# Step sizes of a state-space stage as two products of rounded parts, the bias added on VectorE and ScalarE

## The reference, cut to what matters

```python
xz = x @ W_in                                  # x is layer-normalised, (8, 224, 512)
xb, z = split(xz, 2)                           # 1024 columns each
xb = silu(sum(xp[:, k:k+L] * conv_w[:, k] for k in range(4)) + conv_b)
dt_low, Bm, Cm = split(xb @ W_x, [64, 80])     # 64 + 16 + 16 columns
dt = softplus(dt_low @ W_dt + b_dt)            # W_dt is (64, 1024): the step sizes
# then: a scan over time with exp(A * dt), dt * xb, B and C; the gate silu(z); W_out;
# a cross-attention layer; a mixture of four experts
```

## Time and profile before

| | |
|---|---|
| three runs, median (range) | 2560.08 us (2556.69 to 2561.12) |
| the profiled execution | 2564.23 us, of which 2562.4 between first and last instruction |
| PE, DVE, ACT, POOL busy over the span | 92%, 58%, 48%, 54% |
| mean granted clock of PE | 0.959 of full |

### The profile page before, as it was taken

How to read it: one execution, slowest core, us unless ns; L and a number is a source line. 1 busy time by engine, 2 the same in 40 slices (tenths; PEclk the granted TensorE clock), 3 DMA queues, 4 the chain that set the end, 5 groups by cost and what they waited for, 6 DMA issues and landing times. The chain is left out here.

```text
span 2562.4 us, 39583 instructions
## 1 busy us (share of the span) xinstructions
PE 2358.7 (92%) x14400; PEld 1994.0 (78%) x14400; DVE 1478.9 (58%) x2051; ACT 1223.5 (48%) x2655; POOL 1378.6 (54%) x968
## 2 busy tenths in 40 slices
PE   6999589999999998789999899885899999999997
PEld 5867389999999996557766666663789999999996
DVE  7804599999999994456666766663422232212322
ACT  4335377778777863334453444442333333323332
POOL 2414378778878783366566556652580080006586
PEclk9999789999999998889999999887899999999999
DMA  4326866666665664655545554621431031002323
GB/s 113 135 66 210 262 199 200 190 187 208 202 203 178 207 204 119 167 125 124 121 122 138 124 138 105 173 67 49 163 131 63 33 143 35 33 16 93 109 74 111
DMA packets 236116, 341.95 MB, mean 133 GB/s; under 512 B 35215, under 2 KB 164815, under 8 KB 234927
## 3 DMA queue, kind: packets, MB, share of 16 engines
q1 hardware_dynamic: 217246, 286.22, 39.5%
q0 software_dynamic: 14624, 50.40, 6.1%
q10 hardware_dynamic: 4080, 3.18, 0.5%
HBM read 212.08 MB, written 127.65 MB: 133 GB/s over the span
## 5 line engine op out<-in xcount | busy, mean ns | idle before, releaser
L975 DVE TENSOR_TENSOR_SCAN s_h<-s_decay,s_ub 128x928 f32<-128x928 f32 x256 | 527.2, 2080 | 8.2 <-PE s_ub L1004 1.6
L1015 PE MATMUL s_yps<-s_hc,identity 128*128 128x224 f32 x2016 | 424.1, 353 | 0.4
L2216 DVE TENSOR_TENSOR e_hl<-e_ps,e_hh 128x256 fp32r<-128x256 f32 x256 | 107.9, 424 | 497.1 <-ACT e_ps L2290 496.0
L894 ACT ACTIVATE s_decay<-s_dt,s_A 128x224 f32<-128x224 f32 x1024 | 388.0, 472 | 0.0
L1359 DVE TENSOR_REDUCE t_nmax<-t_ps 112x1 fp32r<-112x752 f32 x256 | 240.1, 938 | 224.8 <-PE t_ps L1700 224.2
L1015 PEld LDWEIGHTS s_yps<-s_hc,identity 128*128 128x128 f32 x2016 | 362.5, 190 | 2.2 <-POOL s_hc L839 1.7
L2289 ACT ACTIVATE e_hh<-e_ps,e_b 128x256 fp32r<-128x256 f32 x256 | 121.8, 476 | 498.3 <-PE e_ps L2325 498.1
L1315 POOL TENSOR_TENSOR t_part<-t_pT 125x672 f32<-125x672 f32 x128 | 207.1, 1618 | 271.8 <-ACT t_pT L1605 269.4
L1605 ACT ACTIVATE t_pT<-t_ps 125x448 f32<-125x448 f32 x384 | 181.1, 546 | 253.9 <-PE t_ps L1726 248.6
L839 POOL TENSOR_TENSOR s_hc<-s_h,carry 128x896 f32<-128x896 f32 x128 | 249.7, 1959 | 75.5 <-DVE s_h L975 51.9
L839 POOL TENSOR_TENSOR s_hc<-s_h,s_Cc 128x896 f32<-128x896 f32 x128 | 248.2, 1947 | 68.3 <-DVE s_h L975 49.8
(11 more groups left out here) (255 smaller groups left out, 5055.4 us busy)
## 6 DMA issues: line engine op xcount, KB each, us to landing
s_ut<-ut_d SPq DMA_DIRECT2D x192, 128.0 KB, 3.3
carry<-in_L_ffn_We POOLq DMA_DIRECT2D x24, 1024.0 KB, 5.7
t_k<-kh_d SPq DMA_DIRECT2D x64, 375.0 KB, 6.3
xs_d<-s_zero SPq DMA_DIRECT2D x30, 512.0 KB, 4.2
ut_d<-a_x SPq DMA_DIRECT2D x31, 448.0 KB, 5.5
kh_d<-s_kh SPq DMA_DIRECT2D x32, 375.0 KB, 2.8
kl_d<-s_kl SPq DMA_DIRECT2D x32, 375.0 KB, 3.3
v_d<-s_v SPq DMA_DIRECT2D x48, 250.0 KB
```

The lines of the kernel that those rows point to most:

```text
L894: ins = nc.scalar.activation(decay[:, u % 2, :, n, 2:SLOT], dts[:, u % 2].rearrange("p (s t) -> p s t", s=NSEG), ACT.Exp, scale=A[:, u % C ...
L975: nc.vector.tensor_tensor_scan(h[:, k].rearrange("p n t -> p (n t)"), decay[:, u % 2, k].rearrange("p n t -> p (n t)"), ub[:, s % 2, AT:AT ...
L1015: ins = nc.tensor.matmul(yps[:, u % 2, 0:L], ident[:], hc[:, u % 2, :, n], start=(n == 0), stop=(n == NS - 1))
```

## The change

`low_rank` now holds 128 rows: the 64 rows rounded to fp32r, and below them their rounded rests. `W_dt` is loaded twice, one copy below the other, rounded into `wdth` (128 rows); the rest of its first 64 rows is `wdtl`. A product is then two fp32r matmuls: `wdth` by all 128 rows (high x high plus high x low), and `wdtl` by the first 64. The row of ones is gone. The bias is a column for each chunk, `bdt`: it is the `bias` of the Abs on ScalarE, which makes two instructions out of one, and VectorE adds it, with the max, by two instructions in place in PSUM before the sum. Some tiles move (`wdt`, `xdbl` and the zeros for padding rows now lie in the space of x), which adds waits.

```diff
-            sp.dma_start(wdt[0:R], W_dt).then_inc(wdt_loaded, 16)
-            sp.wait_ge(wdt_zeroed, 1)
-            sp.dma_start(wdt[R:R + 1].rearrange("o (c p) -> o c p", p=P), b_dt.rearrange("p (o c) -> o c p", o=1),
-                         allow_slow_non_contiguous=True).then_inc(wdt_loaded, 16)
+            sp.dma_start(bdt[:], b_dt).then_inc(wdt_loaded, 16)
+            sp.wait_ge(zeroed, 1)
+            for n in range(2):
+                sp.dma_start(wdt[n * R:(n + 1) * R], W_dt).then_inc(wdt_loaded, 16)
...
-            nc.vector.memset(wdt[R:TT], 0.0).then_inc(wdt_zeroed, 1)
...
             dve.wait_ge(xn_done, NT)
-            nc.vector.memset(low_rank[R:R + 1], 1.0).then_inc(ones_set, 1)
+            nc.vector.memset(zeros, 0.0).then_inc(zeroed, 1)
             for n in range(UNITS):
                 convolution(n)
+            dve.wait_ge(wdt_loaded, 16 * 3)
+            nc.vector.tensor_copy(wdth[:], wdt).then_inc(wdt_high, 1)
+            dve.wait_ge(wdt_high, 1)
+            nc.vector.tensor_tensor(wdtl[:], wdt[0:R], wdth[0:R].bitcast(F32), ALU.subtract).then_inc(wdt_split, 1)
             for half in range(2):
-                dve.wait_ge(xdbl_mm, 2 * half + 2)
-                nc.vector.tensor_copy(grouped(xdbl[:, half_rows(half)]), ps[0:XR, 4 + 2 * half:6 + 2 * half, 0:GL]).then_inc(xdbl_done, 1)
+                both = ps[:, 4 + 2 * half:6 + 2 * half, 0:GL]
+                dve.wait_ge(low_high, half + 1)
+                nc.vector.tensor_tensor(grouped(low_rank[R:2 * R, half_rows(half)]), both[0:R],
+                                        grouped(low_rank[0:R, half_rows(half)].bitcast(F32)), ALU.subtract).then_inc(low_done, 1)
+                nc.vector.tensor_copy(grouped(xdbl[:, half_rows(half)]), both[0:XR]).then_inc(xdbl_done, 1)
...
             def softplus(j):
+                cs, rows = item(j)
                 dve.wait_ge(dt_mm, j + 1)
+                for i in range(2):
+                    nc.vector.tensor_scalar(ps[:, DT_BANK + i, 0:GL], ps[:, DT_BANK + i, 0:GL], bdt[:, cs.start + i:cs.start + i + 1], 0.0,
+                                            ALU.add, ALU.max).then_inc(relu_done, 1)
+                dve.wait_ge(relu_done, 2 * j + 2)
                 dve.wait_ge(ln_done, j + 1)
-                nc.vector.scalar_tensor_tensor(out=grouped(steps[j % RING]), in0=banks(DT_BANK), scalar=0.0, in1=grouped(steps[j % RING]),
-                                               op0=ALU.max, op1=ALU.add).then_inc(dt_done, 1)
+                nc.vector.tensor_tensor(grouped(steps[j % RING]), banks(DT_BANK), grouped(steps[j % RING]), ALU.add).then_inc(dt_done, 1)
 
             def turned_inputs(j):
+                if j == 1:
+
+                    dve.wait_ge(pads_stored, 16 * 8)
+                    dve.wait_ge(cs_stored, 16 * 2)
...
-                nc.scalar.activation(grouped(steps[j % RING]), banks(SIZE_BANK), ACT.Abs).then_inc(abs_done, 1)
+                c = item(j)[0].start
+                for i in range(2):
+                    nc.scalar.activation(steps[j % RING][:, i * GL:(i + 1) * GL], ps[:, SIZE_BANK + i, 0:GL], ACT.Abs,
+                                         bias=bdt[:, c + i:c + i + 1]).then_inc(abs_done, 1)
...
             for half in range(2):
-                act.wait_ge(xdbl_done, half + 1)
+                act.wait_ge(xdbl_mm, 2 * half + 2)
...
-                    ins = nc.tensor.matmul(ps[:, bank + i, 0:GL], wdt[:, c * P:(c + 1) * P], low_rank[:, rows], start=True, stop=True)
+                    of = slice(c * P, (c + 1) * P)
+                    nc.tensor.matmul(ps[:, bank + i, 0:GL], wdth[:, of], low_rank[:, rows], start=True, stop=False)
+                    ins = nc.tensor.matmul(ps[:, bank + i, 0:GL], wdtl[:, of], low_rank[0:R, rows], start=False, stop=True)
...
-            pe.wait_ge(wdt_loaded, 32)
-            pe.wait_ge(ones_set, 1)
+            pe.wait_ge(wdt_split, 1)
             pe.wait_ge(low_done, 2)
+            pe.wait_ge(xdbl_done, 2)
             pe.wait_ge(z_done, 2)
             size(0)
```

More of the change, by code:

```diff
@@ L83, in sem @@
             return sems[-1]
-        x_sb = sb("x", [TT, NT, DM])
+        with nc.sbuf_tensor("a_low_rank", [P, T], F32R) as low_rank:
+            pass
+        x_all = sb("x", [P, NT, DM])
+        x_sb = x_all[0:TT]
         xn = sb("xn", [TT, 2, DM])
@@ L100, in mamba_in @@
         wx_step, step7 = sb("wx", [P, TH]), sb("step7", [P, TH])
-        xdbl = sb("xdbl", [XR, T])
-        wdt = sb("wdt", [TT, DI])
+        wdth, wdtl, bdt = sb("wdth", [P, DI], F32R), sb("wdtl", [R, DI], F32R), sb("bdt", [P, CC])
         ps = ctx.enter_context(nc.psum_tensor("a_ps", [P, 8, 512], F32))
         wx = wx_step[:, 0:CC * XR].rearrange("p (c n) -> p c n", n=XR)
-        x_flat = x_sb[:].rearrange("p n d -> p (n d)")
-        low_rank = x_flat[:, 0:T]
-        uth, utl = (x_flat[:, T + i * UT_RING * DI:T + (i + 1) * UT_RING * DI].rearrange("p (j t) -> p j t", t=DI)
+        x_flat = x_all[:].rearrange("p n d -> p (n d)")
+        wdt, zeros = x_flat[:, T:T + DI], x_flat[0:PAD, T + DI:T + 2 * DI]
+        xdbl = x_flat[0:XR, T + 2 * UT_RING * DI - T:T + 2 * UT_RING * DI]
+        uth, utl = (x_flat[0:TT, T + i * UT_RING * DI:T + (i + 1) * UT_RING * DI].rearrange("p (j t) -> p j t", t=DI)
                     for i in range(2))
@@ L125, in mamba_in @@
         xb_stored, z_stored = sem("xb_stored"), [sem(f"z_stored{i}") for i in range(2)]
-        xdbl_mm, xdbl_done, low_done, ones_set, wdt_zeroed, cs_stored = (
-            sem(n) for n in ("xdbl_mm", "xdbl_done", "low_done", "ones_set", "wdt_zeroed", "cs_stored"))
+        xdbl_mm, xdbl_done, low_high, low_done, zeroed, wdt_high, wdt_split, cs_stored = (
+            sem(n) for n in ("xdbl_mm", "xdbl_done", "low_high", "low_done", "zeroed", "wdt_high", "wdt_split", "cs_stored"))
         bt_mm, bt_high, bt_split, bt_stored, pads_stored = (
             sem(n) for n in ("bt_mm", "bt_high", "bt_split", "bt_stored", "pads_stored"))
-        size_mm, dt_mm, abs_done, exp_done, ln_done, dt_done, u_done = (
-            sem(n) for n in ("size_mm", "dt_mm", "abs_done", "exp_done", "ln_done", "dt_done", "u_done"))
+        size_mm, dt_mm, abs_done, exp_done, ln_done, relu_done, dt_done, u_done = (
+            sem(n) for n in ("size_mm", "dt_mm", "abs_done", "exp_done", "ln_done", "relu_done", "dt_done", "u_done"))
         ut_mm, ut_high, ut_split = ([sem(f"{n}{i}") for i in range(2)] for n in ("ut_mm", "ut_high", "ut_split"))
@@ L170, in _ @@
             sp.dma_start(wx, W_x.rearrange("(c p) n -> p c n", p=P)).then_inc(wx_loaded, 16)
-            sp.dma_start(wdt[0:R], W_dt).then_inc(wdt_loaded, 16)
-            sp.wait_ge(wdt_zeroed, 1)
-            sp.dma_start(wdt[R:R + 1].rearrange("o (c p) -> o c p", p=P), b_dt.rearrange("p (o c) -> o c p", o=1),
-                         allow_slow_non_contiguous=True).then_inc(wdt_loaded, 16)
+            sp.dma_start(bdt[:], b_dt).then_inc(wdt_loaded, 16)
+            sp.wait_ge(zeroed, 1)
+            for n in range(2):
+                sp.dma_start(wdt[n * R:(n + 1) * R], W_dt).then_inc(wdt_loaded, 16)
             for part in range(2):
                 for rows in (slice(0, 2), slice(T + 2, T + PAD)):
-                    zeros = wdt[TT - PAD:TT - PAD + rows.stop - rows.start]
-                    sp.dma_start(ut_d[part, rows], zeros).then_inc(pads_stored, 16)
-                    sp.dma_start(bt_d[part, rows], zeros[:, 0:NS]).then_inc(pads_stored, 16)
+                    some = zeros[0:rows.stop - rows.start]
+                    sp.dma_start(ut_d[part, rows], some).then_inc(pads_stored, 16)
+                    sp.dma_start(bt_d[part, rows], some[:, 0:NS]).then_inc(pads_stored, 16)
             for c in range(CC):
@@ L440, in _ @@
             for half in range(2):
-                act.wait_ge(xdbl_done, half + 1)
+                act.wait_ge(xdbl_mm, 2 * half + 2)
                 nc.scalar.activation(grouped(low_rank[0:R, half_rows(half)]), ps[0:R, 4 + 2 * half:6 + 2 * half, 0:GL],
-                                     ACT.Copy).then_inc(low_done, 1)
+                                     ACT.Copy).then_inc(low_high, 1)
+            act.wait_ge(wdt_loaded, 16 * 3)
             gates(2)
```

6 lines of the change are left out of this document (3 added, 3 removed).

## The result

| | before | after |
|---|---|---|
| median (range), same chip | 2560.60 us (2556.69 to 2562.70, 4 runs) | 2577.93 us (2575.73 to 2586.20, 4 runs) |
| the profiled execution | 2564.23 us, span 2562.4 | 2579.71 us, span 2577.8 |
| mean granted clock of PE | 0.959 | 0.952 |
| the scan stage begins | 304.65 us | 326.12 us |

After / before is 1.0077 [1.0053, 1.0101]. The forecast was 2550.5 us.

A forecast was written before the change was run, and what follows sets the result against it. PE was taken to bound the input stage's third part, then DVE and DMA; cheaper products less DVE pairs, with DMA's queue at the end, gave a lead of 9.5 us from 2560.1, so 2550.5 us, range 2546.5 to 2557.

The forecast's parts named there:

- the price of the products: PE, each size or step: four fp32r products take 0.82 us instead of 1.50, saving 0.68, 32 times.
- the products gain less: Rival, chance 0.10: 64 and 128 rows in turn cost more than 0.82; at 1.5 the kernel takes 2566 us.
- The structure of the sum: Input stage's path: 23 savings of 0.68 us (15.8, with what is lost to ACT) less six DVE pairs (7.6).
- six DVE pairs: DVE's two bias-and-max instructions before a sum, six times on the path, each adding 1.26 us.
- lead: How much sooner than before a place in the input stage is reached; 9.9 us at its end, taken as 9.5.
- The period of the run: Items without gates near the input stage's end: DVE's sums stand 4.65 us apart instead of 3.39.
- The clock: Rival, chance 0.22: idle gaps halve PE's clock, costing up to 1.7 us at some gates; 2554 us at the middle.
- neither bound, 0.75 or 2.2: DVE pair's price limits: 0.75 us if as in SBUF, 2.2 if each instruction costs a whole 896-column one from PSUM.
- The ACT pair: ACT, each item: two Abs of 448 columns take 0.98 us instead of 0.919 for one, 0.06 more.
- The cover at 152: Before the third part: DVE's copy of xdbl ends at 150.6, 1.5 us ahead of PE's need at 152.08.
- DMA, the term that set the forecast's end: End of input stage: DMA's queue, 11 transfers from 275.0, ends at 292.05 against 301.9, a lead of 9.9 us.

The follow-up runs named there:

- e5: Changed kernel with the low product on 96 or 112 rows, zeros below the 64; medians 2554.11 us (96) and 2545.15 us (112), no ratio.
- e10: e1 with each high product issued three times, the first two overwritten; 2568.35 us, ratio 1.0030 to the kernel before.
- e3: Kernel before with its fp32 products and only the bias moved, to DVE and ACT; 2571.07 us, ratio 1.0038.
- e1: Changed kernel with the low product padded from 64 to 128 rows by zeros, same result; 2551.76 us, ratio 0.9964 to the kernel before.
- e8: e1 with eight more filler products in each of items 9 to 12; 2551.52 us, ratio 0.9964 to the kernel before.
- e2: Changed kernel with the old Abs and old max-and-sum, bias left out, so only the products change; 2568.26 us, ratio 1.0030 to the kernel before.
- e11: The changed kernel again, unedited, with more rounds and a second trace; 2582.64 us, ratio 1.0082 to the kernel before.
- e6: Changed kernel with each item issuing both 128-row products first, then both 64-row ones; median 2565.56 us, no ratio.
- e9: Changed kernel with both products on 64 rows, leaving out high times low_rank's rest; median 2562.97 us, no ratio.
- e4: e2 with the low product on 128 rows, bias left out; 2544.13 us, ratio 0.9933 to the kernel before.
- e7: Changed kernel with a 128-row low product carrying the bias in its spare rows, old Abs and sum; 2547.85 us, ratio 0.9956 to the kernel before.

## Why the prediction was wrong

**The step that failed** is the price of the products: "Four fp32r ones of the same 448 columns should go at the distance of the gates' matmuls". That distance was read between matmuls of 128 rows, and of 112 rows and 128. It was carried over to 64 and 128 in turn, which the trace of before doesn't hold. 0.82 us was 1.60. The prediction named the case ("the products gain less", chance 0.10), with the right mechanism, the load of the stationary operand showing between them, and dismissed it because 112 and 128 follow each other at 0.21. e5 confirms that observation, and for 96 too; it just doesn't extend to 64. The rival's price was capped at "as now", 1.5; nothing excluded a loss on PE itself.

The Trainium skill, "TensorE: Matmul & The Clock Gate", section "Step-by-step: what each phase is for", says that PE pulls a load of weights ahead of running matmuls if the row groups don't conflict or if it goes to the background buffer, and that the load's duration doesn't depend on the rows. The trace agrees with the duration (0.18 and 0.19 us). The pulling ahead it shows for equal heights and for 96 or 112 beside 128, and not for 64 beside 128. Why the hardware does so no run shows.

**The structure of the sum held.** It was 23 savings on the path less six DVE pairs. (23 x 0.68 is 15.6, not the 15.8 of the rival's text; the forecast doesn't hang on it.) With an item of 1.64 that gives 23 x (1.50 - 1.64) - 7.6 = -10.8; e10, at full clock, has its next stage 9.7 late and its ratio says 7.7. With 1.50 (e3) it gives -7.6, where 9.3 and 9.7 were measured, three falls of the clock among them. With 0.82 (e1) the forecast was 2550.5, 9.5 us below before, and the measurement 2551.76, by its ratio 9.2 below. Step by step in e1: gates(6) at 179.41 (lead 2.8, forecast 2.4), behind a Silu with 1.72 us of idle PE before it, as foreseen; gates(9) at 207.18 (5.1, forecast 5.4); gates(12) at 234.96 (8.6, forecast 8.9); first sum of the run at 253.25 (10.4, forecast 10.3). The period of the run was 4.71 (4.65). The closeness of single places is in part luck: the trace of e1 is the fastest of its twelve runs, and of the 24.4 us between it and the trace of before only 7.0 lie in this stage.

**The clock** was a rival, rightly placed for e1 and too small for the changed kernel. In e1 the run's gaps let it fall:

```profile
260.00:265.00 5.00, 4.11 (x14) 2.97 (x13) 4.96 (x9) 1.13 (x1) 2.40 (x2) 0.50 0.93 295
265.00:270.00 5.00, 5.00 (x17) 4.45 (x17) 3.43 (x5) 0.00 (x0) 2.40 (x2) 0.60 0.95 298
```

The gates behind the run start slow. Item 13's sum still leads by 6.4, as worked out (10.3 less three pairs); item 15's should lead by 7.2 + 0.68 - 1.26 = 6.6 and leads by 3.5. That is 3.1 us, within the prediction's "up to 1.7 us at gates 14 and 15 each", though at gates 14 alone it was 2.3 (e8 against e1). In the changed kernel the clock falls six times, and that is worth about 12 us (after against e10). The prediction sought the cause in gaps, that is in idle time, and priced it at 1.7 us for each gates. Gaps alone don't account for it: e10 waits as long for the same sums and stays at 1.00, and in e2 at 194 the clock fell with PE busy throughout and no wait. The falls do mostly stand behind waits, in kernels without products of 64 rows too. Counted from 150 us to the end of PE's work, one trace each, the clock is slow in six stretches in after, e11, e6 and e9, which have 64 rows; in two, three, four and five in e1, e8 and e5 with 96 and with 112 rows; and in none in e10. e9, where 64 rows follow 64 with no load exposed, has each of its last five falls within 3 us behind a wait of 1.25 to 1.67 us, so it doesn't part small products from gaps. Whether it is the few rows, the exposed loads or just fewer matmuls in the same time that lowers the clock isn't shown. The Trainium skill, in the same page, Part 1, says that the clock follows how busy PE has been. That fits only if "busy" is not what the profile counts: from 280 to 300 us the changed kernel counts as busy for 18.79 us and e10 for 16.92, and the first has 0.57 where the other has 1.00.

**What the loss consists of**, from ratios, in us. Bias on DVE and ACT: +9.7 (e3), or 7.9 between e1 and e4. Products with all of 128 rows: -17 (e4). 64 rows instead of 128: +29 (e1 to after), of which 17 is length (e1 to e10; 23 x (1.60 - 0.82) = 18) and 12 clock. Taken as a chain, before to e4 to e1 to after, -17 + 8 + 29 = +20 is 1.0077 (19.7) by construction and tests nothing; that the bias alone costs 9.7 from before (e3) and 7.9 from e4 to e1 does agree within the intervals.

**The other terms.** The DVE pair costs 1.31 (predicted 1.26), each instruction 0.686 us for 448 columns (predicted 0.64); neither bound, 0.75 or 2.2, was near. The ACT pair costs 0.24 more and not 0.06: with its bias operand an Abs of 448 is 0.631 where the copy that I took was 0.538. Its effect was hardly more than PE's wait of 1.25 us, not 1.01, before size(3). The cover at 152 held:

```profile
149.67 1.09 DVE L351 COPY a_x<-a_ps 96x896 f32<-96x896 f32 x1
```
```profile
152.30 0.37 PE L539 MATMUL a_ps<-a_low_rank,a_wdth 128*128 128x448 f32 x1
```

The copy ends at 150.76, predicted 150.6, and PE comes without waiting. DMA, the term that set the forecast's end, isn't reached in the changed kernel: its share is 0.23 in 300 to 305. It is reached in e7, where it takes back 3.7 us, and in e4, where it takes back nothing.

## What to carry to other kernels

- A matmul's price is a property of its neighbours as well. Before a stationary operand is made smaller, look in the trace for the exact pair of row counts in turn; if it isn't there, the load of 0.19 us may be exposed at each change, which here doubled the price of an item (0.82 to 1.60 us). Padding to 128 rows with zeros cost nothing on PE here (0.205 us apart, as 64 rows behind 64 are), and the spare rows can do work (here the bias).
- Add up savings and costs by what stands on the path, as done here, and ask for each unit price whether a row of the same shape and the same neighbours shows it. Here the DVE pair, from a row of another width, came out at 1.31 for 1.26 and held; the ACT pair, from a copy without a bias, at 0.24 for 0.06, which hardly mattered; and the products, from rows with other neighbours, at 1.60 for 0.82. That term was the largest.
- A small rival whose only counter-evidence is a neighbouring case deserves its full price: here 0.78 us times 23, and the clock besides.

## What the runs showed of the hardware

- Between a matmul of 128 rows and one of 64, in either direction, 0.20 us is added at full clock (448 columns, fp32r). None between 64 and 64, 96 and 128, or 112 and 128.
- The granted clock can fall to 1.2 GHz while PE is busy in every window and waits for nobody, behind a stream of 64 and 128 rows in turn (e2 at 194 us, one trace; the changed kernel has the same stream at 190 to 195 without a fall); twice the matmuls of 128 rows in the same time kept it at 2.4 GHz throughout, even at 156 to 160 where it fell before (e10).
- Where it falls differs between executions of a kernel and between kernels of equal time (e1 and e8), and moves the end of this stage by 5 to 9 us in a single trace.
